# A four-layer graph network on one Trainium2 core: the sync engine waits for scattered groups itself, and a fifth of the sorting sends moves into the ranking stage

## What is computed

```python
edge_index = stack([src, dst])
x = layernorm(x + gcn(x, edge_index))            # sum of scaled x[src] into dst, batch statistics
x = layernorm(x + capsules(x, edge_index))       # 4 rounds of routing over the edges
x = layernorm(x + transformer(x, edge_index, edge_attr))
#   inside: out = zeros.at[src].add(messages) @ Wo; x = x + out; x + relu(norm(x) @ W1 + b1) @ W2 + b2
x = layernorm(x + mean_layer(x, edge_index))     # out = (sum of x[src] into dst + x) / (deg + 1), @ W.T, mixed, normed
```

## Time and profile before

| | us |
|---|---|
| median of 3 runs | 5265.04 (5263.86 to 5271.49) |
| the profiled execution's own time | 5274.68 |
| its span, first to last instruction | 5272.9 |
| busy PE / DVE / ACT / POOL | 3360.3 / 3707.9 / 2381.2 / 2918.3 |
| mean granted TensorE clock | 0.832 |

### The profile page before, as it was taken

The page is one execution under the profiler, slowest core; times in us unless marked ns, Lnnn a source line. Parts: engine busy times, 40 slices in busy tenths (PEclk is TensorE's granted clock), DMA queues, the critical chain, the costliest instruction groups (busy, mean ns, idle before and its releaser), DMA issues. The chain is left out here.

```text
span 5272.9 us, 70797 instructions
## 1 busy us (share of the span) xinstructions
PE 3360.3 (64%) x20489; PEld 2676.9 (51%) x20592; DVE 3707.9 (70%) x10180; ACT 2381.2 (45%) x5571; POOL 2918.3 (55%) x2733
## 2 busy tenths in 40 slices
PE   6888855277612377653166653555999993875664
PEld 1455544277601255543166652333777772775663
DVE  8877777299834476632277767886888883775887
ACT  6444400199800165532123222553666662333887
POOL 2577577345577433247777745774777655304700
PEclk9999987599955599975588876887999997998887
DMA  5666688299857778742267635884555553886874
GB/s 219 182 187 194 174 309 291 76 298 318 252 183 262 244 261 280 245 138 80 74 196 259 206 92 166 280 281 148 172 185 186 183 174 109 259 252 204 278 247 168
DMA packets 684357, 1095.96 MB, mean 208 GB/s; under 512 B 108888, under 2 KB 451979, under 8 KB 677722
## 3 DMA queue, kind: packets, MB, share of 16 engines
q1 hardware_dynamic: 580772, 908.27, 52.9%
q0 software_dynamic: 103200, 183.16, 11.6%
HBM read 664.33 MB, written 439.19 MB: 209 GB/s over the span
## 5 line engine op out<-in xcount | busy, mean ns | idle before, releaser
L2240 PE MATMUL ro_end<-vals,end_mask 128*2 128x128 f32 x1600 | 236.9, 312 | 378.9 <-DVE vals L2104 275.6
L2366 POOL DMA_INDIRECT sc_rows<-layer,node_idx x400 | 391.5, 979 | 124.4 <-issue 121.6
L719 POOL DMA_INDIRECT agg<-late_agg_sent,d_last x200 | 218.1, 1091 | 324.9 <-issue 299.0
L2240 PEld LDWEIGHTS ro_end<-vals,end_mask 128*2 128x2 f32 x1600 | 146.1, 95 | 461.4 <-DVE vals L2104 286.7
L2972 ACT ACTIVATE tf_hidden<-tf_h_ps,pre_b 128x512 f32<-128x512 f32 x392 | 268.8, 687 | 227.3 <-PE tf_h_ps L3012 216.8
L2266 PE MATMUL ro_acc<-vals,ro_mask 128*126 128x128 f32 x1600 | 245.4, 318 | 187.2 <-ACT ro_square L2198 140.4
L3024 PE MATMUL tf_o_ps<-pre_w,tf_hidden 128*128 128x128 f32 (+1 forms) x3136 | 358.1, 275 | 0.0
L1599 POOL DMA_INDIRECT cap_own<-layer,w_own x200 | 205.0, 1025 | 273.9 <-SPq L1579 221.1
L3024 PEld LDWEIGHTS tf_o_ps<-pre_w,tf_hidden 128*128 128x128 f32 (+1 forms) x3136 | 353.9, 192 | 0.5 <-issue 0.5
L3012 PE MATMUL tf_h_ps<-tf_x_t,pre_w 128*128 128x512 f32 x784 | 348.2, 597 | 9.4 <-ACT tf_hidden L2972 8.2
L2054 POOL TENSOR_TENSOR vals<-ro_both,ro_weight 126x1024 f32<-126x1024 f32 x75 | 144.9, 1932 | 342.2 <-ACT ro_weight L2222 252.3
(11 more groups left out here) (493 smaller groups left out, 10984.9 us busy)
## 6 DMA issues: line engine op xcount, KB each, us to landing
ro_mask<-masks SPq DMA_DIRECT2D x100, 504.0 KB, 4.7
layer<-zeros SPq DMA_DIRECT2D x96, 512.0 KB
si_both<-layer SPq DMA_DIRECT2D x48, 1024.0 KB, 6.0
ro_far<-far SPq DMA_DIRECT2D x75, 512.0 KB, 6.2
ro_both<-both SPq DMA_DIRECT2D x75, 512.0 KB, 6.0
agg<-zeros SPq DMA_DIRECT2D x48, 512.0 KB
mom_x<-in_x_dram SPq DMA_DIRECT2D x48, 512.0 KB, 8.8
mom_agg<-agg SPq DMA_DIRECT2D x48, 512.0 KB, 7.5
```

Of the source, the lines that this page charges most:

```text
L719: pool.indirect_dma_start(out=self.dest, out_offset=bass.IndirectOffsetOnAxis(ap=self.order.last_idx[:, t:t + 1], axis=0), in_=self.sent[: ...
L2240: mm = nc.tensor.matmul(end_ps[0:2, j, :], k.end_mask[:, t, :], k.vals[:, t, :], start=True, stop=True, skip_group_check=True)
L2366: nc.gpsimd.indirect_dma_start(out=rows[:, g % SC, c * GT + j, :], out_offset=None, in_=k.layer1, in_offset=bass.IndirectOffsetOnAxis(ap=k ...
```

## The change

There are two parts.

In the ranking stage the rank is finished group by group (`ranks`), and POOL's list gets a third entry: in its last ten steps (m from 40 to 49) it sends payload group m - 40. `send_payloads` in the moments stage is left with groups 10 to 49, and group g now waits until `used` is (g - 10) * 49 / 40.

In the transformer and in the last stage ACT's `ready` goes. SP reads `needs` into a register and waits for `arrived` itself, right before the load of msum (or agg). The waits for free buffers move ahead of the first load of a pair, and in the last stage own is now loaded before agg.

```diff
+PG = 10
@@ rank_and_sum_phase, gpsimd
+                def payload(m):
+                    g = m - (EG - PG)
+                    if g >= 0:
+                        pool.wait_ge(s["ranked"], g + 1)
+                        send_payload(k, pool, g)
-                pipeline(EG, (gather, 0), (scatter, 3))
+                pipeline(EG, (gather, 0), (scatter, 3), (payload, 0))
@@ rank_and_sum_phase, vector
-                pipeline(T, (hots, 0), (twins, 0), (picks, 2), (masks, 2))
-                dve.wait_ge(s["twinned"], T)
-                dve.wait_ge(s["rank_picked"], T)
-                nc.vector.tensor_tensor(rank[:, :], parts[:, 0, :], parts[:, 1, :], ALU.add).then_inc(s["ranked"], 1)
-                dve.wait_ge(s["ranked"], 1)
+                def ranks(n):
+                    if n % GT != GT - 1:
+                        return
+                    at = slice(n - GT + 1, n + 1)
+                    dve.wait_ge(s["twinned"], n + 1)
+                    dve.wait_ge(s["rank_picked"], n + 1)
+                    nc.vector.tensor_tensor(rank[:, at], parts[:, 0, at], parts[:, 1, at], ALU.add).then_inc(s["ranked"], 1)
+
+                pipeline(T, (hots, 0), (twins, 0), (ranks, 3), (picks, 2), (masks, 2))
+                dve.wait_ge(s["ranked"], EG)
@@ send_payloads
-    for g in range(EG):
-        if g >= 2:
-            pool.wait_ge(k.scattered[RF + g % 2], sent(g - 2))
-            pool.wait_ge(used, min(g - 1, NG + 1))
+def send_payload(k, pool, g):
+    if g >= 2:
+        pool.wait_ge(k.scattered[RF + g % 2], payload_sent(k, g - 2))
+    for t in range(g * GT, (g + 1) * GT):
+        k.nc.gpsimd.indirect_dma_start(
+            out=k.sorted4[:, :], out_offset=bass.IndirectOffsetOnAxis(ap=k.rank[:, t:t + 1], axis=0),
+            in_=k.payload[:, t, :], in_offset=None).then_inc(k.scattered[RF + g % 2], 16)
+    for g in range(PG, EG):
+        if g > PG:
+            pool.wait_ge(used, min((g - PG) * (NG + 1) // (EG - PG), NG + 1))
+        send_payload(k, pool, g)
@@ transformer_phase, sync
-                    sp.dma_start(x2[0:p, u, :, :], node_rows(k.x2, n, p)).then_inc(s[f"x2_in{u}"], 16)
-                    if n >= TL:
                         sp.wait_ge(s["normed"], n - TL + 1)
                         sp.wait_ge(s["rest_made"], n - TL + 1)
-                    sp.wait_ge(s["ready"], n + 1)
+                    sp.dma_start(x2[0:p, u, :, :], node_rows(k.x2, n, p)).then_inc(s[f"x2_in{u}"], 16)
+                    groups = sp.value_load(late.needs[0:1, n:n + 1], min_val=1, max_val=EG)
+                    sp.wait_ge(s["arrived"], groups)
                     sp.dma_start(msum[0:p, u, :, :], node_rows(k.msum, n, p)).then_inc(s[f"msum_in{u}"], 16)
@@ both stages, scalar: goes, with its calls
-                def ready(n):
-                    if n <= NG:
-                        groups = act.value_load(late.needs[0:1, n:n + 1], min_val=1, max_val=EG)
-                        paced(act, k, s["arrived"], groups)
-                        act.sem_inc(s["ready"], 1)
@@ mean_layer_phase, sync
                 def load_agg(n):
-                    if n >= ML:
-                        sp.wait_ge(s["turned"], 2 * (n - ML + 1))
-                    sp.wait_ge(s["ready"], n + 1)
+                    groups = sp.value_load(late.needs[0:1, n:n + 1], min_val=1, max_val=EG)
+                    sp.wait_ge(s["arrived"], groups)
                 def load_own(n):
                     if n >= ML:
+                        sp.wait_ge(s["turned"], 2 * (n - ML + 1))
                         sp.wait_ge(s["z_made"], n - ML + 1)
-                pipeline(NG + 1, (load_agg, 0), (load_own, 0), (load_shifted, 2), (store, 6))
+                pipeline(NG + 1, (load_own, 0), (load_agg, 0), (load_shifted, 2), (store, 6))
```

More of the change, by code:

```diff
@@ L1496, with payload_sent @@
 CS = 4
-def send_payloads(k, pool, used):
-    def sent(g):
-        return k.scatter_base[RF + g % 2] + g // 2 * 16 * GT + 16 * GT
-    for g in range(EG):
-        if g >= 2:
-            pool.wait_ge(k.scattered[RF + g % 2], sent(g - 2))
-            pool.wait_ge(used, min(g - 1, NG + 1))
[L1508 to L1511, removed]
+def payload_sent(k, g):
+    return k.scatter_base[RF + g % 2] + g // 2 * 16 * GT + 16 * GT
+def send_payload(k, pool, g):
[5 more added lines that the diff above has]
+            in_=k.payload[:, t, :], in_offset=None).then_inc(k.scattered[RF + g % 2], 16)
+def send_payloads(k, pool, used):
+    for g in range(PG, EG):
+        if g > PG:
+            pool.wait_ge(used, min((g - PG) * (NG + 1) // (EG - PG), NG + 1))
+        send_payload(k, pool, g)
     for g in range(EG - 2, EG):
-        pool.wait_ge(k.scattered[RF + g % 2], sent(g))
+        pool.wait_ge(k.scattered[RF + g % 2], payload_sent(k, g))
     for g in range(EG):
@@ L2811, in transformer_phase @@
         names = (["xm_made", "lifted", "rest_made", "normed", "turned", "x_copied", "hidden_made", "bent", "out_made", "x3_added",
-                  "x3_made", "stored0", "stored1", "w_step", "w_made", "indexed", "landed", "arrived", "ready",
+                  "x3_made", "stored0", "stored1", "w_step", "w_made", "indexed", "landed", "arrived",
                   "moved", "moved_put0", "moved_put1"]
@@ L2945, in _ @@
             def _(act):
-                def ready(n):
-                    if n <= NG:
-                        groups = act.value_load(late.needs[0:1, n:n + 1], min_val=1, max_val=EG)
-                        paced(act, k, s["arrived"], groups)
-                        act.sem_inc(s["ready"], 1)
-                for n in range(TL):
-                    ready(n)
                 act.wait_ge(s["w_step"], 2)
@@ L2983, in root @@
                     return lambda n: norms[m].square_root(act, n, n % 2, tail(n))
-                pipeline(NG + 1, (lambda n: ready(n + TL), 0), (back, 2), (front, 1), (finish, 4), (root(1), 3), (root(0), 0))
+                pipeline(NG + 1, (back, 2), (front, 1), (finish, 4), (root(1), 3), (root(0), 0))
             @block.tensor
@@ L3155, in mean_layer_phase @@
         names = (["turned", "turned_copied", "z_made", "normed", "gained", "added", "res_made", "stored0", "stored1",
-                  "arrived", "ready"] + [f"{x}_in{u}" for x in ("agg", "own", "shifted") for u in range(ML)])
+                  "arrived"] + [f"{x}_in{u}" for x in ("agg", "own", "shifted") for u in range(ML)])
         s = {x: k.sem(st, "ml_" + x) for x in names}
@@ L3249, in finish @@
                     norms[1].normalise_on_act(act, n, u, p, res[:, u, :, :], total[:, u, :, :]).then_inc(s["res_made"], 1)
[L3251 to L3260, removed]
+                pipeline(NG + 1, (copy, 0), (normalise, 3), (finish, 5),
                          (lambda n: norms[0].square_root(act, n, n % 3, tail(n)), 2),
```

## The result

The changed kernel takes 5252.7 us in the median of 9 runs (5249.9 to 5263.35), the kernel before 5268.93 beside it (9 runs, 5263.49 to 5292.98). The ratio is 0.9973, with a 95% interval of 0.996 to 0.9985: 14 us faster by the ratio and 16 by the medians, where -17 was forecast.

What follows compares the result with a forecast made beforehand. No engine bounds it throughout: POOL's sends end moments, PE bounds the transformer, a two-block loop slows the last stage. Terms -46 + 14 + 0 - 10 + 16 + 9 = -17 give 5248 us against the median 5265.04; range 5228 to 5272.

Steps and rivals of the forecast that it cites:

- Sends out of moments, -46: Moments stage: 20 sends instead of 56 run alone at its end, 36 fewer at 1.27 us, so 46 us less.
- Sends into ranking, +14: Ranking stage: forty sends at 1.32 us take 53 us, POOL's idle time covers 39, and 14 stick out.
- The rival in which ranking pays in full: Ranking stage, chance 0.08: POOL's idle time can't be used, so 53 us come on top; 5287 us.
- The bound of 1.58 us a send for contention: Ranking stage: moved sends as dear as beside DVE's work in moments, making the ranking term 24 us.
- Transformer, 0: Transformer: 6.6 us of cover before PE hides SP's added waits of 1 to 2 us, so no cost.
- Start of the last stage, -10: Last stage's start: ACT's first copy no longer waits for block 3's groups; 10 us earlier, bounds -5 and -12.
- Last block, +9: Last stage's end: own goes first in the block of 106 partitions, so agg comes 8.85 us later.
- Steps of the last stage, +16: Last stage's loop over two blocks: agg 0.9 us late each turn, 0.75 us a pair over 22 pairs.
- The prediction's own sign of error: Last stage: the prediction called itself wrong if the gap between own and agg on SP was above 1 us.
- the prediction's bounds of 4 and 20 us: Last stage's steps: the 22 pairs lose at least 4 us, with a stalled share of 0.21, and at most 20.
- the rival that the loop has room: Last stage's steps, chance 0.25: agg's delay is hidden, steps keep 8.62 us or reach 8.39; 5226 to 5236 us.
- The rival of a dear register load: Last stage, chance 0.17: each us of SP's register load above 0.5 costs 22 us; at 2.7, 5296 us.

Runs made afterwards that it cites:

- the run with agg first: Changed kernel with agg loaded ahead of own again in the last stage, register read still right before agg; 0.9932 of the kernel before, 44 steps 381.5 us.
- the last-block run: Changed kernel with agg loaded ahead of own in the last block alone; one run, 5253.12 us, 44 steps 396.1 us, rest 53.3.
- own first: Changed kernel, own still ahead of agg, with the next block's register read moved behind agg; one run, 5249.96 us, 44 steps 390.9 us.
- agg first, the read ahead: Changed kernel with agg ahead of own and the next block's register read behind own; 0.9929 of the kernel before, 44 steps 375.3 us.

## Why the prediction was right, point by point

*Sends out of moments, -46*: -46.7, and -43.5 to -51.4 over the ten profiles with 10 groups, all against the one profile of the kernel before. Its step, 36 sends fewer in the quiet end at 1.27 us, is seen in the windows, and the run with 7 groups puts them back at this price.

*Sends into ranking, +14*: +15.9, and +11.8 to +16.3 over the same ten. 53 us of sends, 39 of them covered: the runs with 7 and 14 groups confirm both the cover and the full price beyond it. The rival in which ranking pays in full falls with them. The bound of 1.58 us a send for contention was not reached: the 40 sends in ranking take 1.03 us on average (0.97 to 0.98 most of them, seven longer, up to 1.4) and a gap of 0.30. Beside that bound the prediction set the rule of the Trainium skill, page "SBUF — State Buffer", section on the two sides of SBUF, that a VectorE instruction with two SBUF inputs and a GpSimd instruction that reads SBUF lock each other out. These sends don't test it: by the tiles that DVE's instructions read, those with two SBUF inputs fill 169 of the 217 us from 708 to 925 in the moments stage, where the DMA share is 0.98, and only 30 of the 115 us from 576.6 to 692 in ranking, where the DMA share is 0.41. Which of the two makes a send dear in moments, no run here separates.

*Transformer, 0*: shown by two runs, 824.7 us with SP's waits and 824.9 without.

*Start of the last stage, -10*: -8.6. The run with agg first gave -12.2. The difference is own ahead of agg, and with it the wait for `z_made` ahead of agg. The agg loads of blocks 3 and 4 are issued 17.1 and 21.5 us after the start of the stage, and 11.4 and 16.3 with agg first; the prediction counted that wait for block 3 only, and put its agg at 14.5.

*Last block, +9*: +9.0, and shown alone by moving one pair of loads. By the rule of the Trainium skill, page "DMA: Bandwidth & Descriptors", section on why a DMA increments its semaphore by 16, that 106 partitions run on 2 engines, the prediction estimated 8.0 us a load; the measured distance of the two loads is 8.79 us.

*Steps of the last stage, +16*: +16.1, but that is luck in part: the step of the prediction behind it was wrong in two sizes that made up for each other, and in which of its two causes counts. It read: "agg is 0.9 us late in each turn of the loop", 0.42 for own's issue and 0.5 for the register load. The issue is late by 1.46 us (1.91 against 0.45). The register load takes its 0.5, own's issue as much, and some 0.5 more arise only when the read stands behind own's issue (on average agg is 0.92 us behind the store with own alone in front, 0.96 with the read alone, 1.91 with both). And the delay of the issue is not the delay of the turn. The prediction equated them: the turn came 0.95 and 1.29 us later in the two profiles, near the 0.9 that it had put there, but not from an issue that was 0.9 us late. Behind agg first, 2.2 us of further delay of the issue moved the turn by 0.5 us and cost nothing; own ahead moved it by 1.1 us for 0.48 of issue, and with it came all of the cost (375.3 to 390.9 us, with the read ahead in both). The prediction's own sign of error, a gap between own and agg above 1 us, did show: it is 1.47 on average. The rest of that step stands: the turn closes the loop over two blocks, the loop has a little room, and a delay beyond it counts. That three quarters of it count for each pair was a choice between the prediction's bounds of 4 and 20 us, and no run shows that share.

So the rival that the loop has room was true of the register load and false of own's place. The rival of a dear register load was false: one behind a store costs 0.50 us, and the loop bears it. With four of them the steps are as slow as with own ahead, with three they are not. (The 200 ns of the Trainium skill, page "Runtime: NRT & Kernel Launch", section on instruction fetch mechanics, are for a register loaded from HBM; `needs` is a tile in SBUF, and its load takes 0.50 us.)

Why agg lands sooner after a late issue is argued, not shown: the store in front and own behind are 512 KB each on the same queue, and an agg issued late finds more of the store gone. That in this stage the load that is waited for first has to be issued first is shown, by the last-block run and by the pair of agg first and own first.

## What to carry to other kernels

Judge a delay of a load by when it lands, not by when it is issued: here up to three register loads in front of a 512 KB load cost nothing that shows, and another 512 KB load in front of it cost some 15 us in 44 steps. Keep the load that is waited for first in front, above all for a partial block, whose two loads are 8.8 us apart here. A combined change of a few tenths of a per cent should be taken apart before it is kept: here, by the profiles, its first part gave 32 us and its second took 17 back. With the order of two loads restored (agg first, the read ahead) the last stage takes 460.1 us, less than in the three profiles with ACT's `ready` (471.8 to 475.4), and the kernel 0.9929 (0.9905 to 0.9954) of the time before. By the profiles both parts are then gains; the timed runs alone can't tell this kernel from the first part alone, 0.9954 (0.9939 to 0.9969).

## What was not expected of the hardware

The first register load on SP behind a store costs 0.50 us, each further one 0.6 to 0.9 (from store to agg 0.96 us with one, 2.68 with three, 3.30 with four), and one behind a load's issue about 1 us (from own to agg 0.48 us without it, 1.47 with it). When store, agg and own are issued one right behind the other, the last of them is long on SP: own takes 0.80 us on average in the kernel before, and 0.51 where three reads stand between store and agg.
